# Waits moved, the last two groups' jobs halved, and the end taken tile by tile, in a sparse graph attention layer

## The chip, the cores and the metric

One NeuronCore of a Trainium2 chip runs the whole kernel. The metric is the device time of one execution in microseconds. A step, a job and a group are words of the kernel and are told below.

## The reference

One transformer layer over a graph of 4096 nodes of 256 features, 8 heads of 32, in float32. The adjacency matrix is very sparse, and its first rows are the fullest.

```python
mask = adj.astype(jnp.float32) + jnp.eye(n)
q, k, v = [(h @ W.T + b).reshape(n, 8, 32) for W, b in ((Wq, bq), (Wk, bk), (Wv, bv))]
scores = jnp.einsum('nhd,mhd->hnm', q, k) / sqrt(32)
scores = jnp.where(mask[None] == 0, -1e9, scores)
ctx = jnp.einsum('hnm,mhd->nhd', softmax(scores), v).reshape(n, 256)
h1 = layer_norm(h + ctx @ Wo.T + bo, ln1_g, ln1_b)
ff = relu(h1 @ W1.T + b1) @ W2.T + b2        # 256 -> 1024 -> 256
return layer_norm(h1 + ff, ln2_g, ln2_b)
```

## The kernel before

The kernel writes tables of k, v and q to DRAM, finds each row's few edges in the adjacency matrix, and gathers only the keys and values of these. The 4096 rows are 32 tiles of 128. They are worked in the order ORDER = [5, 6, 4, 3, 2, 7, 1, 0] of groups of four tiles. One pass over one or two tiles is a **step**: steps 0 to 11 take two tiles each, steps 12 to 15 the single tiles 4 to 7, and steps 16 to 18 the tiles 1, 2 and 3, whose rows are fuller. Tile 0 (TILE0), the fullest, has no step of its own: its pieces are set beside steps 2 to 16 (the functions with a 0 in their name). Its weighted sum sum0_pe stands in step 16 (SUM0).

In a step, VectorE (DVE) multiplies gathered keys and queries (edge_scores_dve, own_scores_dve), masks them, normalizes (norm_probs_dve, which signals own_probs), and weights and adds the values (own_sum_dve, edge_weight_dve). In between it prepares later steps: find_dve searches a tile of the adjacency, two steps ahead (FIND_INDEX8, L493), and starts_dve, rt_dve, cols_dve and onehot_dve make the lists of the next step. Small matmuls move data between rows and slots: starts_pe, lists_pe, ell_pe, tr_pe, sum_pe. ACT makes the distances (distance_act) from which rt is made, and the exponentials. POOL issues the gathers (gather_aligned, gather_edges), which are DMAs by index. SP issues plain loads and stores, among them one adjacency tile of 2 MB for each search (load_adj), into two buffers in turn.

The second half of the layer is done in **jobs**, one for each finished group: attn (post_pe_attn: output projection and residual), statistics (post_dve_stats), the rstd on POOL, the norm on ACT (post_act_norm), h1 (transposes), eight blocks f of ff (matmul, then a relu on ACT), out (eight matmuls and a residual for each tile), statistics and norm again, and gain, final (POOL) and the store. A job of four tiles works beside the steps of the next group; step_of_job gives a step's job, its place in the group and the group's number of steps. ff_gap, outs_own and outs_before say which parts of a job's matmuls stand in which of six gaps (dense(0) to dense(5)) of a step. So job 5 is spread over steps 12 to 15 and job 6 over steps 16 to 18. The last group makes two jobs of two tiles, b and c, which are done mostly after step 18. Every engine runs its instructions in the order in which the code lists them; an instruction that waits holds up all behind it on its engine.

The end of every engine's program is general(): it waits for a flag and for all stores, reads the flag, and skips a slow path that handles rows with too many edges.

```python
eng.wait_ge(flag_ready, 1)
eng.wait_ge(main["stored"], GROUPS * 16)
eng.wait_ge(JOBS[GROUPS]["stored"], 16)
raised = eng.value_load(flag[0:1, 0:1], min_val=0, max_val=1)
```

## Time and profile before

| | us |
|---|---|
| median of 3 runs (lowest, highest) | 646.56 (646.11, 647.59) |
| the profiled execution | 645.0 |
| its span, from the first to the last instruction | 643.2 |
| before step 0's first product | 96.2 |
| steps 0 and 1, to the start of step 2 | 47.4 |
| steps 2 to 11 | 272.2 |
| steps 12 to 15 | 87.4 |
| from step 16 to the last matmul | 125.1 |
| after the last matmul | 14.9 |

A step is taken to start with its first VectorE product (L584). PE is TensorE, PEld its weight loads, DVE is VectorE, POOL is GpSimd. A float32 matmul shows as two records, so x8 is four matmuls. An operation's idle time before it is followed by what ended it: the engine, the tile written and the line.

### The profile page before, as it was taken

The numbers are of one execution on the slowest core, as the hardware profiler recorded it, in microseconds if no ns is written. First come the engines' busy times: TensorE is split into PE (matmuls) and PEld (weight loads), VectorE is DVE, ScalarE is ACT, GpSimd is POOL, SyncE is SP. The second block draws the span as 40 slices with busy tenths as digits, with TensorE's granted clock in tenths as the row PEclk, the third lists the DMA queues.
The fourth block names the chain that finished last, engine by engine and source line by source line (L and its number), as shares of the span: only waits on it lengthen the run. The fifth ranks groups of instructions, "written<-read, shape, count | busy, mean of one in ns | idle before, by whom it ended". The sixth has DMA issues, their size and how long they took to land.

```text
span 643.2 us, 7652 instructions
## 1 busy us (share of the span) xinstructions
PE 525.8 (82%) x2434; PEld 414.5 (64%) x2434; DVE 480.3 (75%) x1210; ACT 169.9 (26%) x357; POOL 242.8 (38%) x370
## 2 busy tenths in 40 slices
PE   4999868966799889799989985897688949799790
PEld 3888657855468558757856862685347847478680
DVE  0788968986898989999999878968989791642000
ACT  1111301221323341252242334214211123222510
POOL 5010233552333355456534332432544351322222
PEclk9999877997799989899989988979857968799897
DMA  8999695995986879787796644165275423110010
GB/s 305 416 425 390 218 371 171 363 385 224 322 310 238 312 264 352 255 304 278 255 353 221 246 139 179 32 218 204 88 270 209 143 73 91 49 34 0 2 49 19
DMA packets 39211, 141.08 MB, mean 219 GB/s; under 512 B 4856, under 2 KB 15352, under 8 KB 35072
## 3 DMA queue, kind: packets, MB, share of 16 engines
q1 hardware_dynamic: 24320, 95.16, 39.9%
q0 software_dynamic: 13328, 43.55, 19.8%
q10 hardware_dynamic: 1520, 1.85, 0.8%
q8 instruction: 21, 0.34, 0.2%
q14 instruction: 22, 0.18, 0.1%
HBM read 123.74 MB, written 16.80 MB: 219 GB/s over the span
## 4 chain that ended last, share of the span: by engine, by line
DVE 45%; PE 35%; issue 9%; ACT 4%; DMA 4%; POOL 3%; SPq 0%; POOLq 0%; DVEq 0%; ACTq 0%
DVE found L493 14%; PE ps L1018 8%; PE ps L1569 6%; PE ps L1030 6%; PE ps L999 5%; PE ps L989 3%; DVE stats L1084 3%; DMA work<-q_table,row_of 2%; DVE slots L683 2%; DVE slots L670 2%; DVE slots L692 2%; PE ps L823 2%; ACT early L1074 1%; PE ps L865 1%; DMA xT_all<-in_xT 1%
## 5 line engine op out<-in xcount | busy, mean ns | idle before, releaser
L1018 PE MATMUL ps<-xT_all,w 128*128 128x512 f32 (+1 forms) x288 | 133.2, 610 | 12.3 <-ACT xT_all L1064 9.9
L493 DVE FIND_INDEX8 found<-ones,adj_buf 128x8 uint32<-128x4105 int32 (+5 forms) x40 | 138.7, 3467 | 0.0
L1030 PE MATMUL ps<-w,xT_all 128*128 128x256 f32 x512 | 122.9, 395 | 6.2 <-ACT xT_all L1064 3.2
L1030 PEld LDWEIGHTS ps<-w,xT_all 128*128 128x128 f32 x512 | 98.9, 198 | 21.6 <-ACT xT_all L1064 5.0
L1018 PEld LDWEIGHTS ps<-xT_all,w 128*128 128x128 f32 x288 | 57.6, 212 | 62.5 <-issue 46.1
L949 POOL DMA_INDIRECT slots<-kv_table,col_of x54 | 54.6, 1010 | 67.6 <-DVE col_of L567 56.0
L1084 DVE BATCH_NORM_STATS2 stats<-ps 128x6 f32<-128x256 f32 x64 | 22.9, 419 | 61.1 <-PE ps L989 61.1
L1064 ACT ACTIVATE xT_all<-ps,col_table 128x512 f32<-128x512 f32 (+1 forms) x72 | 45.5, 641 | 82.5 <-PE ps L1018 76.5
L1569 PE MATMUL ps<-early,xT_all 128*128 128x256 f32 x256 | 57.6, 387 | 9.3 <-DMA xT_all<-in_xT 9.3
L1569 PEld LDWEIGHTS ps<-early,xT_all 128*128 128x128 f32 x256 | 49.5, 194 | 16.2 <-issue 9.3
L823 PE MATMUL ps<-work,slots 128*128 128x128 f32 x160 | 33.8, 318 | 27.2 <-DVE slots L692 25.3
L1102 POOL TENSOR_TENSOR rstd<-mv,eps_col 128x4 f32<-128x4 f32 (+1 forms) x18 | 6.0, 331 | 127.2 <-DVE mv L1090 127.2
L941 POOL DMA_INDIRECT slots<-kv_table,found x32 | 34.9, 1089 | 46.5 <-DVE found L493 15.3
L823 PEld LDWEIGHTS ps<-work,slots 128*128 128x128 f32 x160 | 27.4, 226 | 30.7 <-DVE slots L692 28.6
L953 POOL DMA_INDIRECT work<-q_table,row_of x40 | 38.1, 952 | 12.9 <-issue 12.9
L893 ACT ACTIVATE xT_all<-ps,col_table 128x256 f32<-128x256 f32 (+1 forms) x38 | 14.4, 431 | 96.9 <-PE ps L824 95.7
L1111 POOL TENSOR_TENSOR early<-early,row_g 128x1024 f32<-128x1024 f32 (+1 forms) x9 | 21.1, 2339 | 47.9 <-DVE slots L692 32.0
L1587 PE MATMUL ps<-early,xT_all 128*128 128x256 f32 x128 | 36.6, 413 | 0.0
L999 PE MATMUL ps<-wo,xT_all 128*128 128x256 f32 x128 | 35.6, 404 | 1.0 <-issue 1.0
L1587 PEld LDWEIGHTS ps<-early,xT_all 128*128 128x128 f32 x128 | 26.9, 210 | 4.5
L824 PE MATMUL ps<-ident,slots 128*128 128x128 f32 x124 | 27.9, 312 | 0.0
L786 PEld LDWEIGHTS ps<-idx_all,work 128*128 128x128 f32 x80 | 13.0, 229 | 19.8 <-DVE work L548 18.8
(165 smaller groups left out, 872.1 us busy)
## 6 DMA issues: line engine op xcount, KB each, us to landing
adj_buf<-in_adj SPq DMA_DIRECT2D x31, 2048.0 KB
xT_all<-in_xT SPq DMA_DIRECT2D x15, 512.0 KB, 21.8
kv_table<-slots POOLq DMA_DIRECT2D x7, 1024.0 KB, 12.1
slots<-kv_table SPq DMA_DIRECT2D x12, 512.0 KB
q_table<-slots POOLq DMA_DIRECT2D x16, 256.0 KB, 8.8
out_dram<-early SPq DMA_DIRECT2D x7, 512.0 KB
q_own<-q_table SPq DMA_DIRECT2D x12, 256.0 KB
slots<-in_adj SPq DMA_DIRECT2D x1, 2048.0 KB, 24.6
```

The costliest lines, as they stand in the source:

```text
L493: last = nc.vector.max_index(dst, ones8[:], part)
L823: nc.tensor.matmul(to, edge_slots(q)[:, c, feats], onehot[q.par][:, c, :], start=(u == 0), stop=False)
L941: nc.gpsimd.indirect_dma_start(to, None, kv_dram, bass.IndirectOffsetOnAxis(ap=idx, axis=0)).then_inc(got_aligned[q.par], 16)
L949: nc.gpsimd.indirect_dma_start(edge_slots(q)[:, u, :], None, kv_dram, bass.IndirectOffsetOnAxis(ap=col_of[q.par][:, u:u + 1], axis=0)).the ...
L953: nc.gpsimd.indirect_dma_start(q_edge[q.par][:, u, :], None, q_dram[q.no // 2], bass.IndirectOffsetOnAxis(ap=row_of[q.par][:, u:u + 1], ax ...
L999: nc.tensor.matmul(to, q["ctxT"][:, k, j * P:(j + 1) * P], wo[:, k, :], start=(k == 0), stop=False)
L1018: last = nc.tensor.matmul(ps[:, q["bank"] + f % 2, 0:q["g"] * P], w1[:, k, f * P:(f + 1) * P], q["h1T"][:, k, :], start=(k == 0), stop=(k ...
L1030: nc.tensor.matmul(to, q["ffT"][:, f, j * P:(j + 1) * P], w2[:, f, :], start=(f == 0), stop=False)
L1064: nc.scalar.activation(q["ffT"][:, f, :], ps[:, q["bank"] + f % 2, 0:q["g"] * P], ACT.Relu, bias=bias_1[:, f:f + 1]).then_inc(q["ff"], 1)
L1084: last = nc.vector.bn_stats(q["stats"][k][:, j, :], tile_out(q, q["bank"] + 2 * k, j))
L1569: last = nc.tensor.matmul(ps[:, kv_bank(i, part), j * D:(j + 1) * D], xT_all[:, c, k, r * P:(r + 1) * P], wqkv[:, k, (1 + part) * D:(2 + p ...
L1587: last = nc.tensor.matmul(to, xT_all[:, c, k, r * P:(r + 1) * P], wqkv[:, k, 0:D], start=False, stop=(k == KC - 1))
```

## The change

- The last two groups that have jobs beside steps are treated alike: group 6 (tiles 4 to 7) makes two jobs of two tiles, in the two halves of the job buffers, each beside two steps (14 and 15, 16 and 17), and group 7 makes job 8 (b, beside step 18 and after) and the last job (c). MAIN = 9 counts the jobs on the main signals. Job 5 of four tiles is now beside steps 12 and 13.
- TensorE: lists_pe of the next step stands between two halves of attn; in the last two steps tr_pe stands before gap 2; sum0_pe stands before sum_pe; step 18 has no ff.
- VectorE: the first statistics of a job stand behind norm_probs_dve.
- ACT: the second norm of a job stands behind distance_act of the next step.
- POOL: gather_edges stands before the q stores of gap 2. In the steps that are "apart" (11, 13 and 15) gain waits for own_probs of that step and final for own_probs of the next, both before gather_edges.
- SP: two adjacency loads wait for step 0's gathers. Q_BEFORE is 6 instead of 4.
- The end: out of job c signals for each tile, and VectorE does its second norm, gain and final itself (last_dve), with one power on POOL (last_pool). The flag is made before that out, and the wait for the stores stands behind the reading of the flag.

```diff
+JOBS = [job(GROUP, GROUP * ORDER[n], 0, POST, main) for n in range(GROUPS - 2)]
+for g, at in ((GROUPS - 2, 0), (GROUPS - 2, 2), (GROUPS - 1, 0)):
+    JOBS.append(job(2, GROUP * ORDER[g] + at, at, POST, main))
+JOBS.append(job(2, GROUP * ORDER[-1] + 2, 2, 0, post_signals("e_")))
...
     act.wait_ge(acc_ps, q.b + 1)
-    if step_of_job(q)[1] == 0:
-        wait(act, main["attn_ps"], q.group)
+    wait(act, main["attn_ps"], ctx_free(q.b))
...
+    if js[0] == 0:
+        pe.wait_ge(ctx_sem, ctx_value)
+        pe.wait_ge(q["x_biased"], n + 1)
+        wait(pe, q["ff"], n * FC)
+    for j in js:
         to = tile_out(q, q["bank"], j)
         for k in range(KC):
...
             pe.wait_ge(q["ff"], (n + 1) * FC)
...
-        to = tile_out(q, q["bank"] + 2, j)
+        to = ps[:, q["bank"] + 2 + j, 0:D] if each else tile_out(q, q["bank"] + 2, j)
         for f in range(FC):
             nc.tensor.matmul(to, q["ffT"][:, f, j * P:(j + 1) * P], w2[:, f, :], start=(f == 0), stop=False)
         last = add_residual(to, q["h1b"], j)
-        if j == q["g"] - 1:
+        if each or j == q["g"] - 1:
             last.then_inc(q["out_ps"], 1)
...
+def last_dve(dve, q, j):
+    y, o, moments, r = ps[:, q["bank"] + 2 + j, 0:D], q["out"][:, j, :], q["mv"][1][:, j, :], q["rstd"][1][:, j:j + 1]
+    dve.wait_ge(q["out_ps"], j + 1)
+    nc.vector.bn_stats(q["stats"][1][:, j, :], y).then_inc(q["link2"], 1)
+    dve.wait_ge(q["link2"], j + 1)
+    nc.vector.bn_aggr(moments, q["stats"][1][:, j, :]).then_inc(q["mv2"], 1)
+    dve.wait_ge(q["mv2"], j + 1)
+    nc.vector.tensor_scalar(r, moments[:, 1:2], EPS, None, ALU.add).then_inc(q["plink2"], 1)
+    dve.wait_ge(q["rstd2"], j + 1)
+    nc.vector.tensor_scalar(o, y, moments[:, 0:1], r, ALU.subtract, ALU.mult).then_inc(q["norm2"], 1)
+    dve.wait_ge(q["norm2"], j + 1)
+    nc.vector.tensor_tensor(o, o, rows["g2"][:], ALU.mult).then_inc(q["mul2"], 1)
+    dve.wait_ge(q["mul2"], j + 1)
+    nc.vector.tensor_tensor(o, o, rows["be2"][:], ALU.add).then_inc(q["final"], 1)
+def last_pool(pool, q, j):
+    r = q["rstd"][1][:, j:j + 1]
+    pool.wait_ge(q["plink2"], j + 1)
+    nc.gpsimd.tensor_tensor(r, r, neg_half[:, 0:1], ALU.pow).then_inc(q["rstd2"], 1)
 def wide(name, g):
...
     with eng.If(raised > 0):
+        eng.wait_ge(main["stored"], MAIN * 16)
+        eng.wait_ge(JOBS[MAIN]["stored"], 2 * 16)
         path(eng)
     eng.wait_ge(flag_ready, 1)
...
 def step_of_job(q):
-    same = [p for p in STEPS if p.group == q.group]
-    return q.group - 1, q.b - same[0].b, len(same)
+    return q.b // 2 - 1, q.b % 2, 2 if q.b < NB - 1 else 1
...
-def count_of(g):
-    return len([p for p in STEPS if p.group == g])
...
+    return 2 * n + 2 if n < MAIN - 1 else NB - 2
+def ctx_free(i):
+    return {NB - 3: MAIN - 2, NB - 2: MAIN - 1}.get(i, i // 2 if i % 2 == 0 and i <= 2 * GROUPS - 4 else 0)
+def finished(q):
+    return step_of_job(q)[0] - 1
+def apart(q):
+    return step_of_job(q)[1] == 1 and finished(q) >= 0 and q.b + 2 < NB and STEPS[q.b + 2].T == 1
+Q_BEFORE = 6
...
-    return ((11,), (), (12, 13), (14,), (15,), ())[gap] if i == 1 else ()
+        return ((6,), (), (7, 8), (9, 10), (11,), ())[gap]
+    return ((12,), (), (13,), (14,), (15,), ())[gap] if i == 1 else ()
...
-        return (((), (), (), (), (), (0, 1)), ((2, 3), (4,), (5, 6, 7), (), (), ()))[place][gap]
-    if count == 3:
-        return (((), (), (), (), (), (0, 1)), ((2,), (), (3, 4), (5,), (), ()), ((6,), (7,), (), (), (), ()))[place][gap]
-    return (((), (), (), (), (), ()), ((0, 1), (), (2, 3), (4,), (), ()), ((5,), (), (6, 7), (), (), ()), ((),) * 6)[place][gap]
+    if count == 1:
+        return ()
+    return (((), (), (), (), (), (0, 1)), ((2, 3), (4,), (5, 6, 7), (), (), ()))[place][gap]
 def outs_own(place, count, gap):
-    if count == 2:
-        return {(1, 3): (0, 1)}.get((place, gap), ())
...
-def outs_before(place, g, gap):
-    if place or g < 2:
+    return {(1, 3): (0, 1)}.get((place, gap), ())
+def outs_before(place, n, gap):
+    if place or JOBS[n - 1]["g"] < GROUP:
         return ()
-    if count_of(g - 1) < 4:
-        return {2: (2,), 3: (3,)}.get(gap, ())
-    return {2: (3,)}.get(gap, ())
+    return {2: (2,), 3: (3,)}.get(gap, ())
 block = ctx.enter_context(nc.Block())
...
     load_own(sp, STEPS[0])
+    sp.wait_ge(got_edges[STEPS[0].par], 2 * STEPS[0].U * 16)
     load_adj(sp, 4)
     load_adj(sp, 5)
...
         if i + 3 < NB:
             for ti in range(STEPS[i + 3].T):
                 load_adj(sp, STEPS[i + 3].h + ti)
         if i == NB - 2:
-            sp.wait_ge(main["attn_ps"], GROUPS - 1)
-            post_load(sp, JOBS[GROUPS - 1], GROUPS - 1, JOBS[GROUPS - 1]["t"])
-            post_load(sp, JOBS[GROUPS], 0, JOBS[GROUPS]["t"])
-        if place == 1 and n >= 1:
+            sp.wait_ge(main["attn_ps"], MAIN - 1)
+            post_load(sp, JOBS[MAIN - 1], MAIN - 1, JOBS[MAIN - 1]["t"])
+            post_load(sp, JOBS[MAIN], 0, JOBS[MAIN]["t"])
+        if i >= 1 and apart(STEPS[i - 1]):
+            m = finished(STEPS[i - 1])
+            post_store(sp, JOBS[m], m, JOBS[m]["t"])
+        if place == 1 and n >= 1 and not apart(q):
             post_store(sp, JOBS[n - 1], n - 1, JOBS[n - 1]["t"])
-    a, b, c = JOBS[GROUPS - 2], JOBS[GROUPS - 1], JOBS[GROUPS]
-    na, nb, ne = GROUPS - 2, GROUPS - 1, 0
+    a, b, c = JOBS[MAIN - 2], JOBS[MAIN - 1], JOBS[MAIN]
+    na, nb, ne = MAIN - 2, MAIN - 1, 0
     post_store(sp, a, na, a["t"])
     post_store(sp, b, nb, b["t"])
-    post_store(sp, c, ne, c["t"])
+    for j in range(2):
+        sp.wait_ge(c["final"], j + 1)
+        sp.dma_start(out_rows[:, c["t"] + j, :], c["out"][:, j, :]).then_inc(c["stored"], 16)
...
             post_pool_rstd(pool, JOBS[n], n, 0)
+        if i >= 1 and apart(STEPS[i - 1]):
+            pool.wait_ge(own_probs, i + 1)
+            post_pool_final(pool, JOBS[finished(STEPS[i - 1])], finished(STEPS[i - 1]))
+        if apart(q):
+            pool.wait_ge(own_probs, i + 1)
+            pool.wait_ge(s_weights, 16 * WEIGHT_DMAS)
+            post_pool_gain(pool, JOBS[n - 1], n - 1)
+        if soon:
+            gather_edges(pool, soon)
         for p in q_pairs(i, 2):
             store_q(p)
-        if soon:
-            gather_edges(pool, soon)
         if 0 <= i - GATHER0 < PIECES0:
             gather_edges(pool, TILE0, (2 * (i - GATHER0), 2 * (i - GATHER0) + 1))
...
             post_pool_gain(pool, JOBS[n - 1], n - 1)
             post_pool_final(pool, JOBS[n - 1], n - 1)
         if place == 0 and n >= 1:
             post_pool_rstd(pool, JOBS[n - 1], n - 1, 1)
...
-    post_pool_rstd(pool, a, na, 1)
     post_pool_gain(pool, a, na)
     post_pool_final(pool, a, na)
     post_pool_rstd(pool, b, nb, 1)
     post_pool_gain(pool, b, nb)
     post_pool_final(pool, b, nb)
-    post_pool_rstd(pool, c, ne, 1)
-    post_pool_gain(pool, c, ne)
-    post_pool_final(pool, c, ne)
+    for j in range(2):
+        last_pool(pool, c, j)
     general(pool, general_pool)
...
         if i == NB - 1:
-            post_act_x(act, JOBS[GROUPS - 1], GROUPS - 1)
-            post_act_x(act, JOBS[GROUPS], 0)
+            post_act_x(act, JOBS[MAIN - 1], MAIN - 1)
+            post_act_x(act, JOBS[MAIN], 0)
         dense(0)
         if i + 1 < NB:
             distance_act(act, STEPS[i + 1])
+        if place == 1 and n >= 1:
+            post_act_norm(act, JOBS[n - 1], n - 1, 1)
         dense(1)
         probs_act(act, q)
         if i == SOFTMAX0:
             probs0_act(act)
         dense(2)
-        if place == 0 and n >= 0:
+        if place == 0 and n >= 0 and i < NB - 1:
             post_act_norm(act, now, n, 0)
         edge_exp_act(act, q)
+        if i == NB - 1:
+            post_act_norm(act, now, n, 0)
         if i == WEIGHTS0:
             edge_exp0_act(act)
-        if place == 0 and n >= 0:
+        if place == 0 and n >= 0 and i < NB - 1:
             post_act_h1(act, now, n)
         dense(3)
-        if i == NB - 1:
-            post_act_norm(act, JOBS[GROUPS - 1], GROUPS - 1, 0)
+        if i == SUM0:
+            ctx0_act(act)
         ctx_act(act, q)
         dense(4)
-        if i == SUM0:
-            ctx0_act(act)
         dense(5)
+        if i == NB - 1:
+            post_act_h1(act, now, n)
         if place == 0 and n >= 0:
             post_act_h1_bias(act, now, n)
-        if place == count - 1 and q.group < GROUPS - 1:
-            post_act_x(act, JOBS[q.group], q.group)
-        if place == 0 and n >= 1:
-            post_act_norm(act, JOBS[n - 1], n - 1, 1)
-    a, b, c = JOBS[GROUPS - 2], JOBS[GROUPS - 1], JOBS[GROUPS]
-    na, nb, ne = GROUPS - 2, GROUPS - 1, 0
-    post_act_h1(act, b, nb)
-    post_act_ff(act, b, nb, range(0, 2))
+        if place == 1 and i // 2 < MAIN - 1:
+            post_act_x(act, JOBS[i // 2], i // 2)
+    a, b, c = JOBS[MAIN - 2], JOBS[MAIN - 1], JOBS[MAIN]
+    na, nb, ne = MAIN - 2, MAIN - 1, 0
+    post_act_ff(act, b, nb, range(0, 3))
     post_act_norm(act, c, ne, 0)
-    post_act_ff(act, b, nb, range(2, FC))
+    post_act_ff(act, b, nb, range(3, FC))
+    post_act_norm(act, a, na, 1)
     post_act_h1(act, c, ne)
-    post_act_h1_bias(act, b, nb)
-    post_act_ff(act, c, ne, range(0, 4))
-    post_act_norm(act, a, na, 1)
+    post_act_ff(act, c, ne, range(FC))
     post_act_h1_bias(act, c, ne)
-    post_act_ff(act, c, ne, range(4, FC))
     post_act_norm(act, b, nb, 1)
-    post_act_norm(act, c, ne, 1)
     general(act, general_act)
 @block.tensor
...
     starts_pe(pe, TILE0)
-    for i in range(1, Q_BEFORE):
+    for i in range(1, 4):
         project_q(i)
     lists_pe(pe, TILE0)
+    for i in range(4, Q_BEFORE):
+        project_q(i)
     starts_pe(pe, b1_)
...
         ell_pe(pe, q)
+        if n == MAIN - 1:
+            pe.wait_ge(ctx0_ready, 1)
         if place == 0 and n >= 0:
-            post_pe_attn(pe, now, n, ctx_ready, job_ctx_ready(n))
-        dense(1)
+            post_pe_attn(pe, now, n, ctx_ready, job_ctx_ready(n), range(now["g"] // 2))
         if soon:
             lists_pe(pe, soon)
+        if place == 0 and n >= 0:
+            post_pe_attn(pe, now, n, ctx_ready, job_ctx_ready(n), range(now["g"] // 2, now["g"]))
+        dense(1)
         if 0 <= i - SCORE0 < PIECES0:
             ell0_pe(pe, i - SCORE0)
         if i == WEIGHTS0:
             tr0_pe(pe)
-        dense(2)
+        if i + 2 < NB:
+            dense(2)
         tr_pe(pe, q)
-        if place == 0 and n >= 0:
+        if i + 2 >= NB:
+            dense(2)
+        if place == 0 and n >= 0 and i < NB - 1:
             post_pe_h1(pe, now, n)
         dense(3)
-        if i == NB - 1:
-            pe.wait_ge(ctx0_ready, 1)
-            post_pe_attn(pe, JOBS[GROUPS - 1], GROUPS - 1, ctx_ready, NB - 2)
-        sum_pe(pe, q)
-        dense(4)
         if i == SUM0:
             sum0_pe(pe)
+        sum_pe(pe, q)
+        if i == NB - 1:
+            post_pe_h1(pe, now, n)
+        dense(4)
         dense(5)
         if i + 2 < NB:
             starts_pe(pe, STEPS[i + 2])
-    a, b, c = JOBS[GROUPS - 2], JOBS[GROUPS - 1], JOBS[GROUPS]
-    na, nb, ne = GROUPS - 2, GROUPS - 1, 0
+    a, b, c = JOBS[MAIN - 2], JOBS[MAIN - 1], JOBS[MAIN]
+    na, nb, ne = MAIN - 2, MAIN - 1, 0
+    post_pe_ff(pe, b, nb, (0, 1))
     post_pe_attn(pe, c, ne, ctx_ready, NB)
-    post_pe_h1(pe, b, nb)
-    post_pe_ff(pe, b, nb, range(FC))
+    post_pe_ff(pe, b, nb, range(2, FC))
     post_pe_h1(pe, c, ne)
-    post_pe_ff(pe, c, ne, range(0, 4))
-    post_pe_out(pe, b, nb, range(2))
-    post_pe_ff(pe, c, ne, range(4, FC))
-    post_pe_out(pe, c, ne, range(2))
+    post_pe_out(pe, b, nb, (0,))
+    post_pe_ff(pe, c, ne, (0, 1))
+    post_pe_out(pe, b, nb, (1,))
+    post_pe_ff(pe, c, ne, range(2, FC))
     pe.wait_ge(flag_link, 3)
     nc.tensor.matmul(ps[:, POST, 0:2], ones_col[:], flag_f[:, 0:1].to_broadcast([P, 2]), start=True, stop=True).then_inc(flag_ps, 1)
+    for j in range(2):
+        post_pe_out(pe, c, ne, (j,), each=True)
     general(pe, general_pe)
 @block.vector
...
             rt_dve(dve, soon)
-        if place == 0 and n >= 0:
-            post_dve_stats(dve, JOBS[n], n, 0)
         masked_dve(dve, q)
...
         norm_probs_dve(dve, q)
+        if place == 0 and n >= 0:
+            post_dve_stats(dve, JOBS[n], n, 0)
         if later:
...
     nc.vector.tensor_tensor(limit[:], limit[:], start_of[:], ALU.subtract).then_inc(flag_link, 1)
-    post_dve_stats(dve, b, nb, 0)
     post_dve_stats(dve, c, ne, 0)
-    post_dve_stats(dve, a, na, 1)
     dve.wait_ge(flag_link, 1)
     t0, t1 = TILE0.u0, TILE0.u0 + TILE0.U
     nc.vector.tensor_tensor(bad[:, 1, 0:t0], found[:, 0:t0, FOUND - 1], limit[:, 0:t0], ALU.is_le)
...
     dve.wait_ge(flag_link, 2)
     nc.vector.tensor_reduce(flag_f[:], flat(bad[:]), AX_X, ALU.max).then_inc(flag_link, 1)
     post_dve_stats(dve, b, nb, 1)
-    post_dve_stats(dve, c, ne, 1)
     dve.wait_ge(flag_ps, 1)
     nc.vector.tensor_scalar(flag[:], ps[:, POST, 0:1], 0.0, None, ALU.is_gt).then_inc(flag_ready, 1)
+    for j in range(2):
+        last_dve(dve, c, j)
     general(dve, general_dve)
```

## Rows read from the trace of the kernel before

**Rows 1.** The page, busy time and share of the span of engines.

```profile
PE 525.8 (82%) x2434; PEld 414.5 (64%) x2434; DVE 480.3 (75%) x1210; ACT 169.9 (26%) x357; POOL 242.8 (38%) x370
```

**Rows 2.** Busy time by stretch; last PEclk, DMA share, GB/s.

```profile
core 0: us, PE busy (x) PEld busy (x) DVE busy (x) ACT busy (x) POOL busy (x), PEclk, DMA share, GB/s
96.20:143.60 47.40, 38.80 (x189) 33.37 (x187) 40.80 (x88) 11.57 (x25) 22.83 (x26) 0.91 0.83 302
143.60:415.80 272.20, 233.65 (x1076) 175.42 (x1076) 248.23 (x553) 82.53 (x165) 118.84 (x125) 0.92 0.71 253
415.80:503.20 87.40, 70.26 (x297) 52.46 (x298) 74.81 (x214) 20.27 (x47) 37.31 (x37) 0.80 0.58 200
503.20:560.10 56.90, 42.16 (x207) 32.48 (x205) 33.77 (x100) 16.04 (x35) 18.68 (x23) 0.82 0.28 81
560.10:628.30 68.20, 61.88 (x310) 51.91 (x310) 15.80 (x47) 20.21 (x46) 18.25 (x22) 0.97 0.06 20
628.30:643.20 14.90, 0.12 (x2) 0.03 (x1) 1.05 (x5) 1.02 (x2) 3.72 (x6) 0.68 0.06 21
```

**Rows 3.** Waits of VectorE, 90 to 143.65: total us, times, longest.

```profile
DVE work L584 <- DMA work<-q_table,row_of: 8.4, 3, 5.0
```

**Rows 4.** The same view, 143.65 to 415.8.

```profile
DVE stats L1084 <- PE ps L989: 8.4, 4, 4.7
DVE work L548 <- ACT work L875: 4.6, 2, 2.6
```

**Rows 5.** The same view, 415.8 to 503.2.

```profile
DVE stats L1084 <- PE ps L989: 5.2, 1, 5.2
```

**Rows 6.** The same view, 503.2 to 628.4, VectorE, then TensorE.

```profile
DVE bad L540 <- PE ps L779: 12.1, 1, 12.1
DVE p_edge L660 <- PE ps L806: 11.7, 2, 6.9
...
PE ps L823 <- DVE slots L692: 9.2, 2, 7.1
```

**Rows 7.** The timeline, ff (L1018) and out (L1030): start us, us.

```profile
383.89 3.68 PE L1018 MATMUL ps<-xT_all,w 128*128 128x512 f32 x8
...
451.02 6.19 PE L1018 MATMUL ps<-xT_all,w 128*128 128x512 f32 x8
...
600.52 3.72 PE L1018 MATMUL ps<-xT_all,w 128*128 128x256 f32 x16 [1.11 <-ACT xT_all L1047]
...
612.15 3.62 PE L1030 MATMUL ps<-w,xT_all 128*128 128x256 f32 x16
```

**Rows 8.** Groups of TensorE's instructions, 415.8 to 503.2, then 503.2 to 560.1.

```profile
L1030 PE MATMUL ps<-w,xT_all 128*128 128x256 f32 x80 | 22.8, 449 | 0.4 <-ACT xT_all L1064 0.4
L1018 PE MATMUL ps<-xT_all,w 128*128 128x512 f32 x32 | 21.9, 842 | 0.0
...
L865 PE MATMUL ps<-work,slots 128*128 128x128 f32 x56 | 8.6, 326 | 0.8 <-ACT xT_all L893 0.8
```

**Rows 9.** The timeline, POOL's gain beside VectorE in step 11; L512 in step 12.

```profile
410.70 2.34 POOL L1111 TENSOR_TENSOR early<-early,row_g 128x1024 f32<-128x1024 f32 x1 [14.00 <-DVE slots L692]
410.73 2.33 DVE L512 CAST aligned_idx<-idx_all 128x2 uint32<-128x2 f32 x1
...
440.40 0.17 DVE L512 CAST aligned_idx<-idx_all 128x2 uint32<-128x2 f32 x1
```

**Rows 10.** The chain that ended last: gathers of steps 0 and 1.

```profile
83.58 12.58 DMA work<-q_table,row_of
...
116.54 3.48 DMA work<-q_table,row_of
```

**Rows 11.** The timeline, POOL: a gather's issue; the last final.

```profile
495.51 0.94 POOL L949 DMA_INDIRECT slots<-kv_table,col_of  x1 [0.30 <-issue]
...
633.21 1.26 POOL L1115 TENSOR_TENSOR early<-early,row_be 128x512 f32<-128x512 f32 x1
```

**Rows 12.** The page, DMA issues: KB each, median us to landing.

```profile
out_dram<-early SPq DMA_DIRECT2D x2, 256.0 KB, 2.2
```

94 lines of the change are left out of this document (41 added, 53 removed).

## The prediction

> **What bounds the kernel now.** First the page: TensorE is busy 82% and VectorE 75% of the span [rows 1], so neither is a plain bound, and the question is which one is waited for where. So next the busy time by stretch, cut at the starts of steps [rows 2]. Steps 2 to 11 take 272.2 us with VectorE busy 248.2 (91%): VectorE sets the pace, TensorE (233.7, 86%) follows closely. Steps 12 to 15 take 87.4 us with 74.8 and 70.3. From step 16 to the last matmul, 125.1 us, VectorE has 49.6 us of work and TensorE 104.0: there TensorE is the bound, and it idles 21.1 us on top. The last 14.9 us hold almost no TensorE work. Then the waits by stretch [rows 3 to 6]: places where the pace is broken, which the new order can mend. Last, single instructions: what a job costs TensorE [rows 7, 8], what a POOL operation does to VectorE [rows 9], the gathers [rows 10, 11] and the end [rows 11, 12].
>
> **The sum has five parts**, against the profiled execution (645.0 us, span 643.2; the median of the runs, 646.56, is 1.6 higher, and the forecast adds that).
>
> **A. Steps 0 and 1.** SP now waits for step 0's edge gathers before it loads two more adjacency tiles, and POOL issues gather_edges before the q stores of gap 2. VectorE waited 8.4 us in three waits for gathers [rows 3], 5.0 of them in step 0, where the last gather landed 12.6 us after its issue; a later one took 3.5 [rows 10]. The 12.6 is a shared DMA: 4 MB of adjacency were loading. Held back, they start some 9 us later, when the first search that needs them is still 10 us away, and 2 MB at the 302 GB/s of this stretch [rows 2] take 7, so that is hidden, by 3 us only. The other two waits (3.4) go with the earlier issue. Q_BEFORE 4 to 6 moves two q pairs in front of step 0, into TensorE time that waited for VectorE; POOL's stores, and behind them step 1's aligned gather, wait for them, but that gather waited for a q store before too. Bounds 3 and 8.4; I take 7.
>
> **B. Steps 2 to 11.** post_dve_stats(…, 0) moves behind norm_probs, so VectorE no longer stands before attn: 8.4 us in four waits [rows 4]. lists_pe(soon) now stands behind half of attn. A tile of it has four records of the form of out (16 take 3.62 [rows 7]) and a residual of 0.4, so 1.3: the half is done 2.6 us after ell, about when VectorE has made rt. What is late instead is h1 (rstd, norm and h1T follow statistics that start after own_probs), and it lands in time in which TensorE waits for edge_weighted. post_act_norm(…, 1) moves behind distance_act: of the 4.6 us for ACT's distance [rows 4] one norm, some 1.9, can go; ff(2, 3) stay in front. The apart rule moves gain and final of step 11 under the search. Before, they ran beside small VectorE operations: the cast L512 took 2.33 us, until L1111 ended, against 0.17 elsewhere [rows 9]; two such blocks are 4.2 us. What can go: 8.4 + 1.9 + 4.2 = 14.5. TensorE would then be busy 91%, and its own lateness stays; I take 12, bounds 4 and 17.
>
> **C. Steps 12 to 15.** Here the split of the jobs works. Costs at full clock [rows 7]: a tile of out 3.62 and the residual, 3.9; one f of a four-tile ff 3.68 / 2 = 1.84, so 14.7 a job; attn 1.3 a tile; h1 about 1. Before, steps 16 to 18 carry one tile of job 5's out (3.9) and all of the four-tile job 6 (6.3 + 14.7 + 15.6): 40.5. After, they carry one two-tile job (18.5) in its place, so 22.0 us of TensorE work go to steps 12 to 15: 70.3 + 22.0 = 92.3 us for 87.4. But there 32 records of 512 columns took 21.9 us [rows 8], 14.7 at full clock, and 80 of 256 took 22.8, 18.1 at full clock: 11.9 us are half clock (6.19 against 3.68 for the same eight [rows 7]; granted clock 0.80 [rows 2]). Work without gaps keeps it up: 80.4, plus some 5 of waits. VectorE: 74.8 busy, less 4.2 of the lock in step 13, plus 1.0 for one more set of statistics. One new wait: in steps 11, 13 and 15 POOL's gathers queue behind own_probs and the 2.3 us gain, in 12, 14 and 16 behind final. In step 15 six gathers of 0.94 + 0.30 [rows 11] end 9.8 us after own_probs and land some 2.5 later; step 16 begins 9.1 after it. Those 3.2 us are about what the freed wait (5.2 [rows 5]) leaves over. I take 0, bounds -8 and +10.
>
> The matmuls of ff are now 256 wide for two more jobs. The rows price this at nothing: 16 records of 256 take 3.72, 8 of 512 take 3.68 [rows 7]. The Trainium skill speaks against it (TensorE: Matmul & The Clock Gate, Back-to-back issue gap: with weight loads about 81 ns at 128 columns, 131 at 512). A straight line puts 256 at 98, an estimate by which two halves cost half as much again. The measured rows decide, and rival 6 is what is left.
>
> **D. Step 16 to the last matmul, 125.1 us.** TensorE's work was 104.0; 22.0 have left: 82.0. Half clock adds little here (sum0's 56 records 8.6 us [rows 8]) and mostly stays. The idle 21.1 was made by order: sum0 ran after sum(16) and before starts (VectorE stood 12.1 us), and ff and out stood before tr in steps 17 and 18 (11.7) [rows 6]. Now sum0 runs while TensorE waited 7.1 us for edge_weighted [rows 6], tr of steps 17 and 18 goes before gap 2, and step 18 has no dense work. What stays idle: step 18's chain of tr, exp, weights, sum and h1 (6), step 16's norm before h1 (3), the joints of the end (4), where norm of job a still stands before out b. 82 + 13 = 95, so 30 less. Bounds 15 (the moved work, with part of it lost to new gaps) and 38.
>
> **E. After the last matmul, 14.9 us** [rows 2]. Before: 6.1 us from 628.3 to the end of final at 634.47 [rows 11], over two tiles and three engines; then store, landing (2.2 [rows 12]), the flag read and branch, 8.7. After: one tile, mostly on VectorE: bn_stats, half of what two tiles took, 0.4, aggregate 0.1, add 0.1, pow 0.6, three operations of 256 columns at 0.4, gaps: 2.8. So 3.3 less. The wait for stored moves behind the flag read, which hides the landing: 2.2. Together 5.5, bounds 3 and 7.
>
> **Sum:** 7 + 12 + 0 + 30 + 5.5 = 54.5; 645.0 - 54.5 = 590.5, and with the 1.6 of the median 592.
>
> **Rivals.**
> 1. TensorE is the bound as soon as VectorE is freed. For it: 86% busy already in steps 2 to 11, more work than time in 12 to 15. Against: much of that excess is clock. B gives 4, D 18 (C's surplus runs into step 16): 7 + 4 + 0 + 18 + 5.5 = 34.5, so 612. Chance 0.22.
> 2. POOL stands in the way. If gathers behind gain and final take 5 us to land rather than 2.5, four steps are late by 2.5 each: 10 us, 602. Or its operations, released by the same instruction as the search, hold the search up as they held the cast: six times 2.3, 606. The Trainium skill has such a rule (SBUF — State Buffer, Who interferes with whom: the first to issue holds the shared pair for its whole instruction), and the cast agrees with it; whether a search is such an operation neither says. Chance 0.13.
> 3. The clock. The granted clock is 0.80 and 0.82 in the two stretches with gaps and 0.97 where TensorE is dense [rows 2]. If it stays near the latter everywhere, C gives 8 and B 17: 579. Chance 0.13.
> 4. Slower: TensorE at its 1.2 GHz level. 174.3 us of work lie between step 12 and the last matmul, some 158 at full clock. If new gaps keep it at half clock all through, it costs 6.19 / 3.68 of that, 265 us, and with 20 of idle 285 against 212.5 now: 72.5 more, 24.5 of it back from A, B and E, so 695. It decides from about 55% of that work at half clock; now it is some 15%. Chance 0.04.
> 5. The waits move and nothing comes of it: VectorE's work is unchanged, and every removed wait comes back as one for TensorE, also at the end. 645 to 648. The idle beside a named order speaks against it. Chance 0.02.
> 6. Half-wide matmuls cost half as much again: 7.3 us over the ff of both jobs (14.7 / 2), 599. Against: 3.72 and 3.68. Chance 0.02.
>
> The forecast itself has 0.44, with 583 to 601 as its own range. The cases span 579 to 612; with the bounds of C and D the range is 575 to 616, and rivals 4 and 5 and the far ends of 1 and 3 lie outside. A measurement of this kernel can tell some 0.2% (1.3 us) from no change: faster 0.94, same 0.02, slower 0.04.
>
> **What would show it.** A: no wait for gathers in steps 0 and 1. B: no wait of the statistics for attn, no 2.3 us casts; steps 2 to 11 in 260 us. C: steps 12 to 15 in 82 to 95, TensorE over 90% busy, clock above 0.9, 2 to 4 us of wait for a gather at step 16. D: the 12.1 and both tr waits gone, 95 us to the last matmul. E: 9 to 10 us after it. Wrong would be a granted clock still at 0.8, searches stretched by POOL, or VectorE waiting for adjacency loads.

## The result and the profile after

The changed kernel takes 619.32 us (617.81 to 622.48, 4 runs) where the kernel before took 647.08 beside it: ratio 0.957, 95% interval 0.952 to 0.962. That is faster by 27.8 us. The forecast was 592.0, with a range from 575 to 616: the sign was right, the gain was half of the 54.5 us forecast.

The page of the kernel after, busy times and granted clock in 40 slices [rows 1]:

```profile
PE 520.4 (84%) x2466; PEld 419.9 (68%) x2466; DVE 475.0 (77%) x1218; ACT 171.8 (28%) x369; POOL 243.2 (39%) x376
...
PEclk9999898987899979989797989877999897978898
```

Busy time by stretch, cut at the same places as before: the start of steps 0, 2, 12 and 16, the last matmul's end, the end [rows 2]:

```profile
91.20:134.14 42.94, 35.63 (x177) 31.47 (x176) 40.63 (x90) 9.06 (x21) 19.52 (x22) 0.92 1.02 405
134.14:411.11 276.97, 235.28 (x1049) 174.51 (x1048) 244.83 (x554) 83.64 (x166) 120.30 (x126) 0.91 0.70 249
411.11:508.12 97.01, 88.58 (x452) 73.06 (x450) 73.73 (x227) 29.65 (x68) 44.08 (x47) 0.93 0.53 181
508.12:610.80 102.68, 81.58 (x429) 71.76 (x427) 47.89 (x140) 30.59 (x75) 34.81 (x47) 0.90 0.19 59
610.80:618.30 7.50, 0.19 (x2) 0.00 (x0) 2.16 (x6) 0.00 (x0) 0.56 (x1) 0.65 0.12 38
```

Set against the parts of the sum (the last column is e16 below, the fastest complete kernel of this study, in its one profile):

| part | forecast | after | best |
|---|---|---|---|
| A, to the start of step 2 | -7 | -9.5 | -9.3 |
| B, steps 2 to 11 | -12 | **+4.8** | -12.4 |
| C, steps 12 to 15 | 0 | **+9.6** | +6.2 |
| D, step 16 to the last matmul | -30 | -22.4 | -22.5 |
| E, behind it | -5.5 | -7.4 | -7.3 |
| sum | -54.5 | -24.9 | -45.3 |

B alone is 16.8 us off, C 9.6 and D 7.6. A and E gave 4.4 more than forecast.

In B, VectorE's work fell by 3.4 us, but the stretch grew. The waits in it, VectorE's first, then TensorE's and ScalarE's (us in total, times, longest):

```profile
DVE stats L1090 <- PE ps L991: 6.7, 5, 3.2
DVE total_p L645 <- issue: 6.3, 2, 3.3
DVE total_p L645 <- ACT scores L883: 5.6, 2, 3.3
...
PE ps L788 <- DVE work L550: 21.2, 8, 4.6
...
ACT xT_all L1070 <- PE ps L1023: 53.7, 32, 6.6
```

Two of them are new: before, TensorE waited 0.3 us for rt in this stretch, and VectorE did not wait for the exponentials (L645, 11.9 us in both rows; that the first is one too is read from its place). ScalarE's wait for ff was 32.4 us before. VectorE's for attn, which the change was to remove, is 6.7 us where it was 8.4. L788 is lists_pe, L550 is rt on VectorE. TensorE now arrives at the lists eight times before rt is there, 21.2 us in all. The timeline of step 9 (an odd step: no attn, so nothing but ell stands ahead of the lists) shows the rest:

```profile
329.91 0.54 PE L800 MATMUL ps<-work 128*128 128x48 f32 x4
...
334.55 0.47 DVE L550 TENSOR_SCALAR work<-work,half 128x128 f32<-128x128 f32 x2
...
335.08 1.03 PE L788 MATMUL ps<-idx_all,work 128*128 128x9 f32 x4 [4.62 <-DVE work L550]
...
335.95 3.76 PE L1023 MATMUL ps<-xT_all,w 128*128 128x512 f32 x4
...
339.75 0.69 ACT L1070 ACTIVATE xT_all<-ps,col_table 128x512 f32<-128x512 f32 x1 [6.56 <-PE ps L1023]
...
340.34 0.31 ACT L883 ACTIVATE scores<-scores 128x144 f32<-128x144 f32 x1
340.68 0.41 DVE L645 TENSOR_REDUCE total_p<-scores 128x16 f32<-128x144 f32 x1 [3.31 <-ACT scores L883]
```

TensorE stands idle from 330.5 to 335.1, then makes the lists and ff 4. Four records of ff 4 take 3.76 us, half the rate of [rows 7] (eight in 3.68). The granted clock, the third value from the end, says why: 1.00 ahead of the pause, 0.50, the 1.2 GHz level, in the lists and ff 4 behind it.

```profile
320.00:330.40 10.40, 10.33 (x42) 6.33 (x42) 10.16 (x27) 4.41 (x8) 4.51 (x8) 1.00 0.97 352
335.08:339.71 4.63, 4.63 (x9) 2.56 (x10) 2.09 (x11) 0.00 (x0) 1.90 (x2) 0.50 0.53 182
```

ScalarE's program has ff 4's ReLU ahead of the exponentials, so these wait too, and VectorE, which had the scores ready at 336.1, gets them at 340.7.

### The profile page after: what moved, and what is told of

Read it like the earlier page. It is cut to its first block, busy times and chain, and to the rows that moved or that the text cites. A ratio compares the mean times of both kernels' runs of the same rounds, so it can differ in the third digit from the quotient of the medians.

```text
span 618.3 us, 7757 instructions
## 1 busy us (share of the span) xinstructions
PE 520.4 (84%) x2466; PEld 419.9 (68%) x2466; DVE 475.0 (77%) x1218; ACT 171.8 (28%) x369; POOL 243.2 (39%) x376
## 4 chain that ended last, share of the span: by engine, by line
PE 45%; DVE 33%; issue 9%; DMA 4%; POOL 3%; ACT 3%; another core or an unknown queue 1%; POOLq 0%; ACTq 0%; SPq 0%; DVEq 0%
PE ps L1023 11%; PE ps L1036 9%; DVE found L495 8%; PE ps L1606 6%; PE ps L1003 4%; DMA work<-q_table,row_of 3%; PE ps L1624 3%; PE ps L991 3%; DVE stats L1090 2%; DVE slots L602 2%; PE ps L788 2%; PE ps L825 2%; PE ps L1622 2%; DVE slots L672 2%; DVE slots L685 1%
## 5 line engine op out<-in xcount | busy, mean ns | idle before, releaser
L1036 PE MATMUL ps<-w,xT_all 128*128 128x256 f32 x512 | 120.8, 391 | 5.5 <-ACT xT_all L1070 2.1
L1023 PEld LDWEIGHTS ps<-xT_all,w 128*128 128x128 f32 x320 | 65.7, 215 | 51.7 <-issue 39.7
L1070 ACT ACTIVATE xT_all<-ps,col_table 128x512 f32<-128x512 f32 (+1 forms) x80 | 47.9, 601 | 98.5 <-PE ps L1023 93.8
L1606 PEld LDWEIGHTS ps<-early,xT_all 128*128 128x128 f32 x256 | 49.5, 195 | 16.0 <-issue 9.2
L1090 DVE BATCH_NORM_STATS2 stats<-ps 128x6 f32<-128x256 f32 x62 | 22.4, 419 | 34.6 <-PE ps L991 34.6
L894 ACT ACTIVATE xT_all<-ps,col_table 128x256 f32<-128x256 f32 (+1 forms) x38 | 14.4, 430 | 110.5 <-PE ps L826 110.5
L1003 PE MATMUL ps<-wo,xT_all 128*128 128x256 f32 x128 | 39.6, 439 | 5.3 <-issue 3.0
L825 PE MATMUL ps<-work,slots 128*128 128x128 f32 x160 | 31.1, 297 | 12.5 <-DVE slots L694 9.9
L1138 POOL TENSOR_TENSOR early<-early,row_g 128x1024 f32<-128x1024 f32 (+1 forms) x9 | 18.3, 2031 | 58.1 <-DVE slots L694 23.9
L788 PE MATMUL ps<-idx_all,work 128*128 128x9 f32 (+1 forms) x80 | 13.4, 279 | 29.4 <-DVE work L550 29.2
L825 PEld LDWEIGHTS ps<-work,slots 128*128 128x128 f32 x160 | 25.0, 207 | 14.2 <-DVE slots L694 11.7
L788 PEld LDWEIGHTS ps<-idx_all,work 128*128 128x128 f32 x80 | 12.3, 221 | 31.5 <-DVE work L550 31.4
L1003 PEld LDWEIGHTS ps<-wo,xT_all 128*128 128x128 f32 x128 | 25.2, 218 | 8.4 <-issue 4.7
## 6 DMA issues: line engine op xcount, KB each, us to landing
xT_all<-in_xT SPq DMA_DIRECT2D x14, 512.0 KB, 22.5
kv_table<-slots POOLq DMA_DIRECT2D x7, 1024.0 KB, 12.1
```

The costliest lines, as they stand in the source:

```text
L788: last = nc.tensor.matmul(lists_out(q)[:, u, :], rt[q.par][:, u, :], lists(q)[:, u, q.A:q.room + 2], start=True, stop=True)
L825: nc.tensor.matmul(to, edge_slots(q)[:, c, feats], onehot[q.par][:, c, :], start=(u == 0), stop=False)
L1003: nc.tensor.matmul(to, q["ctxT"][:, k, j * P:(j + 1) * P], wo[:, k, :], start=(k == 0), stop=False)
L1023: last = nc.tensor.matmul(ps[:, q["bank"] + f % 2, 0:q["g"] * P], w1[:, k, f * P:(f + 1) * P], q["h1T"][:, k, :], start=(k == 0), stop=(k ...
L1036: nc.tensor.matmul(to, q["ffT"][:, f, j * P:(j + 1) * P], w2[:, f, :], start=(f == 0), stop=False)
L1070: nc.scalar.activation(q["ffT"][:, f, :], ps[:, q["bank"] + f % 2, 0:q["g"] * P], ACT.Relu, bias=bias_1[:, f:f + 1]).then_inc(q["ff"], 1)
```

## The experiments

Every ratio is to the kernel before, run beside it on the same chip. B, C, D are the stretches above, from one profiled execution of each kernel. The same kernel gave 0.926 on one chip and 0.931 on another (e10 and e16), so a difference of 3 us between two experiments says little.

### The lists back, the norm back, and single parts

e1_lists_back:

```diff
-if place == 0 and n >= 0: post_pe_attn(..., range(now["g"] // 2))
-if soon: lists_pe(pe, soon)
-if place == 0 and n >= 0: post_pe_attn(..., range(now["g"] // 2, now["g"]))
+if place == 0 and n >= 0: post_pe_attn(pe, now, n, ctx_ready, job_ctx_ready(n))
 dense(1)
+if soon: lists_pe(pe, soon)
```

> The changed kernel with one part undone: attn whole, then gap 1, then lists_pe of the next step, as before. Theory 1 (lists_pe in front of half of attn and of ff 4 makes TensorE wait for rt, 21.2 us in steps 2 to 11, drops its clock, and so holds ff 4's relu, which stands before the exponentials on ACT, and the second half of attn): VectorE's waits for the exponentials (11.9 us) and the statistics (6.7 us) in steps 2 to 11 shrink to below 4 us together, TensorE's wait for rt to below 5, and the kernel takes 600 to 608 us against 619. Theory 2 (the norm that now stands before the exponentials on ACT holds them): the waits for the exponentials stay, 615 to 620.

Measured: 602.36 us, ratio 0.933 (0.926 to 0.941): 17 us less than the changed kernel. B takes 263.9, TensorE waits 3.1 us for rt in it, and VectorE's wait for the exponentials is gone. Step 9 in its timeline:

```profile
320.41 0.54 PE L800 MATMUL ps<-work 128*128 128x48 f32 x4
...
320.79 1.95 PE L1023 MATMUL ps<-xT_all,w 128*128 128x512 f32 x4
...
324.29 0.61 PE L788 MATMUL ps<-idx_all,work 128*128 128x9 f32 x4 [1.55 <-DVE work L550]
...
325.33 0.32 ACT L883 ACTIVATE scores<-scores 128x144 f32<-128x144 f32 x1 [1.04 <-DVE scores L638]
```

The same ff 4 fills the gap, takes 1.95 us, and the exponentials wait for nothing but VectorE.

e2_norm_back puts ScalarE's second norm back to the end of the even step (`post_act_norm(act, JOBS[n - 1], n - 1, 1)` behind `post_act_x` at place 0).

> The changed kernel with another part undone: the second norm of a job stands at the end of the first step of a pair on ACT, not behind distance_act of the second. Theory 1: the exponentials are held by ff 4's relu and not by the norm, so the waits for them stay near 12 us, VectorE waits for distance_act again by some 2 us a time, and the time is 619 to 626 us. Theory 2: the waits for the exponentials go, 608 to 613.

Measured: 618.98 us, 0.954 (0.950 to 0.960), no change from 619.3, and VectorE's wait for the exponentials stays:

```profile
DVE total_p L645 <- ACT scores L883: 11.8, 4, 3.3
```

The norm on ScalarE is not what holds them.

e3_lists_alone: the kernel before with the same order of attn, lists and gap 1 and nothing else.

> The kernel before with one part of the change alone: lists_pe of the next step between two halves of attn and before gap 1. Theory 1: TensorE waits for rt in the second step of each pair (4 to 5 us, then ff 4 at half clock) and VectorE for what follows: slower than before by 5 to 15 us, 652 to 662. Theory 2: nothing of note, 643 to 649.

Measured: 671.50 us, 1.038 (1.031 to 1.045), slower than before, and by more than expected, 24 us. Its waits in B:

```profile
DVE stats L1087 <- PE ps L989: 21.6, 5, 6.5
DVE total_p L643 <- ACT scores L881: 10.0, 4, 3.3
...
PE ps L786 <- DVE work L548: 17.5, 8, 4.6
```

With the statistics still ahead of the masking, VectorE also waits for the second half of attn, 4.3 us a group. The order is worst there. That the changed kernel's late statistics hide part of it is the likely reading; the changed kernel has other parts too.

e4_stats_alone: the kernel before with `post_dve_stats(dve, JOBS[n], n, 0)` behind `norm_probs_dve`.

> The kernel before with another part alone: the first statistics of a job behind norm_probs_dve. The forecast's step B: VectorE's waits for attn (8.4 us in steps 2 to 11, 5.2 in step 12, 3.0 in step 16) nearly vanish, and since TensorE idles 13 us before sum_pe in steps 2 to 11 most of it is gained: 632 to 638. Rival (TensorE is the bound as soon as VectorE is freed): the waits come back at starts_pe and tr_pe, 643 to 647.

Measured: 643.07 us, 0.994 (0.991 to 0.997): 4.1 us, less than half of what was expected, and what the rival said. Waits in B, TensorE's and VectorE's:

```profile
PE ps L1008 <- ACT xT_all L1074: 16.5, 5, 5.0
DVE slot_of L556 <- PE ps L786: 6.8, 3, 5.3
```

The 8.4 us of [rows 4] went to the next thing that attn makes late, the lists behind it, and to h1, which waits for a norm whose statistics start later.

### GpSimd's order

e5_gather_first is e1 with gather_edges ahead of gain and final in the apart steps:

```diff
+if soon: gather_edges(pool, soon)
 if i >= 1 and apart(STEPS[i - 1]): ... post_pool_final(...)
 if apart(q): ... post_pool_gain(...)
-if soon: gather_edges(pool, soon)
```

> The first experiment's order (lists behind attn and the first gap), and GpSimd issues the gathers of the step after next ahead of the pending gain and final of a group, in place of behind them. Theory G (the gathers of the last steps are late because they stand behind these two and behind their waits): the 8.0 us that VectorE waited for gathers at the starts of three of the steps 14 to 17 go to under 3, and the time from 602.4 to 595 to 599. Rival (TensorE is the bound there, VectorE's wait is only where its slack shows): the waits for gathers go, waits for TensorE take their place, 601 to 604.

Measured: 606.41 us, 0.936 (0.932 to 0.941), against e1's 0.933. The wait for gathers from step 12 on fell from 8.0 to 2.4 us and nothing came of it. TensorE's waits, e1's row and then this kernel's:

```profile
PE ps L825 <- DVE slots L694: 4.5, 2, 3.5
```

```profile
PE ps L825 <- DVE slots L694: 9.6, 4, 3.5
```

TensorE's wait for VectorE's weighted values (L825 is sum_pe) grew by 5.1 us in its place. The late gathers cost nothing that can be measured here.

e6_apart_off is e1 with `apart()` always False.

> The first experiment's order, and GpSimd makes gain and final of every group at the old place, so that none is held for the next step's softmax to end. If that placing is worth what the prediction gave it (three norms of about 4.2 us of VectorE's wait for GpSimd saved each), the gathers come in time (8.0 us back) but 12.6 come in waits of VectorE beside GpSimd's work: 605 to 608. Rival (the placing costs as much as it saves, since it is what holds the gathers): 601 to 604 or less.

Measured: 612.23 us, 0.944 (0.940 to 0.949): 9.9 us slower than e1 by the medians, 7 by the ratios, and above the range expected. The gathers come in time, as in e5, where that won nothing. Step 11 alone takes 34.8 us, in e1 30.7. The cast of [rows 9] is back, twice, 2.34 and 2.33 us long (min, median, max in ns):

```profile
L514 DVE CAST aligned_idx<-idx_all x7: 169/169/2336, 366.3 to 520.8; 128x2 uint32<-128x2 f32 x5, 128x3 uint32<-128x3 f32 x2
```

In the kernel after, gain and final run beside searches, and the searches are not held: final beside one of step 14 for 1.2 us, gain beside one of step 15 for nearly all of it, and in step 12 a search that began while final was running. The forms of these searches took 2560 and 1227 ns on average before.

```profile
429.06 2.35 POOL L1142 TENSOR_TENSOR early<-early,row_be 128x1024 f32<-128x1024 f32 x1
...
430.98 1.23 DVE L495 FIND_INDEX8 found<-ones,adj_buf 128x8 uint32<-128x1032 int32 x1
...
474.16 2.56 DVE L495 FIND_INDEX8 found<-ones,adj_buf 128x8 uint32<-128x2312 int32 x1
475.54 2.35 POOL L1142 TENSOR_TENSOR early<-early,row_be 128x1024 f32<-128x1024 f32 x1
...
495.88 2.56 DVE L495 FIND_INDEX8 found<-ones,adj_buf 128x8 uint32<-128x2312 int32 x1
...
495.98 2.35 POOL L1138 TENSOR_TENSOR early<-early,row_g 128x1024 f32<-128x1024 f32 x1 [4.70 <-DVE scores L657]
```

### Start, end, and all but the split

e7_start_alone: the kernel before with part A (`sp.wait_ge(got_edges[...], ...)` ahead of the adjacency loads, gather_edges ahead of store_q, `Q_BEFORE = 6`).

> The kernel before with the change's start alone: the load queue waits for step 0's gathers before adjacency, gathers ahead of the q stores, six q pairs before the start with two of them behind the lists. In the changed kernel steps 0 and 1 were over 9.4 us sooner; if that comes from this part alone and is kept to the end, 636 to 640. Rival (what the start wins, steps 2 to 15 give back, as their waits are for TensorE): 643 to 646.

Measured: 635.61 us, 0.981 (0.976 to 0.985), 11.6 us. Nothing is given back later: B takes 271.1 and C 87.5 us, as before.

e8_end_alone: the kernel before with part E (last_dve, last_pool, a store for each tile, the flag read ahead of the wait for stores).

> The kernel before with the change's end alone: the last group's out, statistics, norm and store tile by tile, and the flag read ahead of the wait for the stores. From the last matmul to the end of the span 14.9 us before and 7.6 in the changed kernel; if it is this part, 639 to 641 and 7 to 8.5 us behind the last matmul. Rival (the shorter tail came from the smaller jobs and their own buffers): 644 to 646.

Measured: 640.58 us, 0.989 (0.984 to 0.994), 6.6 us; 7.3 us are left behind the last matmul.

e12_all_but_split: both and e4 together, four-tile jobs to the end, lists at the old place.

> The kernel before with the change's start, statistics and end together, groups of four tiles up to the end and the lists at the old place. If the three add (11.6, 4.1 and 6.6 us measured alone): 623 to 627, and what the first experiment has beyond it, 21 to 25 us, is the split of the last groups with the order of the last steps. Rival (the parts win the same waits): 629 to 633.

Measured: 623.00 us, 0.964 (0.960 to 0.967). The three add up: 22.3 us alone, 23.5 together (the kernel before took 646.5 beside it). So e1's remaining 20.6 us are the split of the jobs with the order of the last steps, ScalarE's norm (nothing by e2) and GpSimd's order, which e6 puts at 7 to 10.

### Where the lists cost

By the starts of steps, after against e1: the even steps 2 to 10 differ by 1.4 us in sum, the odd ones 3 to 11 by 11.7. Two kernels take the places apart:

```diff
 # e9_whole_attn            # e10_gap_back
 post_pe_attn (whole)       post_pe_attn (half 1)
 lists_pe                   lists_pe        if attn here
                            post_pe_attn (half 2)
 dense(1)                   dense(1)
                            lists_pe        if no attn here
```

> The changed kernel with attn whole in front of the lists, the lists still in front of the first gap's ff. Changed kernel against the first experiment by step starts: the even steps 2 to 10 differ by 1.4 us in sum, the odd steps 3 to 11 (no attn there, ff 4 in the gap) by 11.7. Theory P (the price is the lists ahead of the gap's ff 4 in the odd steps, which goes half clock and holds ReLU and exponentials): little won here, 614 to 618. Rival (the halves of attn, as the prediction placed the risk, start the delay that the odd steps only show): 603 to 607. Both in part: 608 to 613.

> The changed kernel with the lists between the halves of attn kept in the even steps, and behind the first gap's ff in the odd steps. Theory P (see the run before): nearly all of the first experiment's 17 us, 603 to 606. Rival (the halves of attn): 614 to 618.

Measured: e9 620.12 us, 0.953 (0.948 to 0.959); e10 600.64 us, 0.926 (0.923 to 0.930). Each lies just outside the range of theory P, on the side away from the rival: the halves of attn cost nothing that can be measured, and the loss comes from the odd steps, where the lists went ahead of ff 4.

e11_stats_first is e1 with the first statistics ahead of masked_dve, as before.

> The first experiment with VectorE's first statistics ahead of the masking, as in the kernel before. Its TensorE waits 16.6 us in five of the steps 2 to 11 for ScalarE's norm, which waits for these statistics; before, VectorE waited 3.6 to 4.7 us a group for attn there. Theory S (the move is worth its 4.1 us alone, no more once the rest is changed): 604 to 608. Rival (without the late lists TensorE is ahead, the statistics find attn done, and the norm comes sooner): 598 to 601.

Measured: 611.02 us, 0.945 (0.942 to 0.949): 8.7 us slower than e1. The move of the statistics, worth 4.1 alone, is worth about twice that with the rest, and neither number expected came out.

e13_ff4_later is the changed kernel with ff 4 in gap 2: `((2, 3), (), (4, 5, 6, 7), (), (), ())`.

> The changed kernel as it is, lists between the halves of attn and ahead of the first gap in both kinds of step, but ff 4 of the odd steps stands in the next gap (behind the exponentials on ScalarE, ahead of the transposes of the probabilities on TensorE), in place of the first. Theory R (the price is ff 4's ReLU, which ScalarE runs ahead of the exponentials and which waits for TensorE, which waits for VectorE): nearly all won, 600 to 606. Rival T (TensorE's wait for rt and its slower clock are the price): 613 to 619.

Measured: 616.47 us, 0.951 (0.946 to 0.955), 3 to 4 us less than the changed kernel. The exponentials come in time now. In its step 9, and among its waits of VectorE in B:

```profile
332.16 1.03 PE L788 MATMUL ps<-idx_all,work 128*128 128x9 f32 x4 [4.63 <-DVE work L550]
...
333.19 0.32 ACT L883 ACTIVATE scores<-scores 128x144 f32<-128x144 f32 x1 [2.91 <-DVE scores L638]
...
334.03 8.21 PE L1023 MATMUL ps<-xT_all,w 128*128 128x512 f32 x16
```

```profile
DVE p_edge L662 <- PE ps L808: 10.8, 4, 3.6
```

What had been a wait for exponentials is one for tr (L808), which now stands behind four blocks of ff. So ScalarE's order is at most a small part of the price: TensorE stands idle with ff 4 ready, has it still to do afterwards, and whichever consumer comes next is late by it.

The idle time by itself is not the price either. In B TensorE waits 15.1 us for rt in e14 below, which has e10's order, and 3.1 in e1, and B is 263.5 and 263.9 us. There the wait stands behind ff 4, not ahead of it.

### Steps 12 to 15 and the last steps

Each of the four runs here starts from e10. e16_same_again is e10 unchanged, run beside e17.

> The last kernel but two (lists behind the gap in the odd steps, 600.6 us) with half of group 5's ff left out: of the two parts of the sum over the model's width only the first is computed for this group, in steps 12 and 13, about 7.2 us of TensorE at full clock. Theory C (TensorE bounds steps 12 to 15, as its 86.7 busy us of 93.9 say): steps 12 to 15 take 87 to 90 us, the time 594 to 597. Rival (VectorE's chain bounds them): under 2 us, 599 to 601.

> The kernel of 600.6 us with the out of the first job of two tiles taken from step 17 (ahead of its weights' sum) to step 18 behind its scores and attn. In step 18 VectorE waited 5.0 us for TensorE's scores behind this out, and TensorE later 3.5 us for the last weights. Theory D (that wait is at the head of the end's chain): TensorE's 3.5 us and part of the others go, 594 to 598. Rival (TensorE's 50 busy us in the last 60 set the end, the waits come elsewhere): 599 to 602.

> The kernel of 600.6 us once more, unchanged, as the measure for the run beside it: 598 to 603.

> The kernel of 600.6 us with half of the ff of group 5 and of the first two jobs of two tiles left out (one of the two parts of the sum over the model's width is not computed for them), 7.2 + 3.6 + 3.6 us of TensorE at full clock in steps 12 to 17. Theory C (TensorE bounds these steps): 8 to 13 us less than the run beside it, steps 12 to 15 at 84 to 88 us. Rival (VectorE's chain or the gathers bound them, TensorE's busy time only filled what was free): 0 to 4 us less. Between them if both stand close to each other: 5 to 7 less.

The edits, e14 with group 5 alone in place of the three, and e15:

```diff
-for k in range(KC):
+kc = 1 if any(q is JOBS[m] and n == m for m in (5, 6, 7)) else KC   # e17
+for k in range(kc):
...
+if n != MAIN - 2: post_pe_out(pe, now, n, outs_own(place, count, gap))          # e15
+if n == MAIN - 1: return {1: (0, 1)}.get(gap, ())          # in outs_before
```

Measured: e14 600.18 us, 0.926 (0.922 to 0.930), not the 594 to 597 of theory C: steps 12 to 15 take 89.1 us, inside its 87 to 90, but the time is that of e10 (0.926) and 3 us under that of e16 (0.931), both on other chips. e16 601.75 us, 0.931 (0.928 to 0.934). e17 596.22 us, 0.921 (0.918 to 0.924), 5.5 less than e16, steps 12 to 15 in 88.2. So 14.4 us less of TensorE's work are worth 5.5: TensorE and VectorE stand close together there, the third case that was expected. e15 604.81 us, 0.931 (0.926 to 0.936), no gain: VectorE's wait of 5.0 us for the scores of step 18 is gone from its trace, but one of 7.1 for tr (1.3 in e16) has come, so it does not show what the wait alone was worth.

e16's stretches 2 to 11, 12 to 15, 16 to the last matmul:

```profile
134.39:394.22 259.83, 223.86 (x1046) 166.16 (x1046) 244.06 (x555) 83.49 (x166) 120.57 (x126) 0.95 0.74 266
394.22:487.78 93.56, 87.86 (x455) 72.32 (x453) 73.49 (x226) 29.58 (x68) 43.68 (x47) 0.95 0.54 187
487.78:590.40 102.62, 81.62 (x428) 71.68 (x427) 47.79 (x140) 30.64 (x75) 35.20 (x47) 0.90 0.19 59
```

This kernel (e10 and e16), 600.6 and 601.8 us in two sets of runs, beats both: 45 us under the kernel before and 18 under the changed one.

## Why the prediction was wrong

**A held, by 2.5 us more.** No wait for gathers is left in steps 0 and 1, and e7 shows it kept to the end.

**B is the step that failed.** The prediction looked at attn alone: "the half is done 2.6 us after ell, about when VectorE has made rt", and went on to h1. Where there is attn that cost nothing (e10), though rt is later than it says: e16's TensorE waits for it there too, up to 2.5 us. But the same line moves the lists ahead of the gap's ff in the odd steps, where nothing stands between ell and the lists, and this was put at nothing. The trace of before had the price: in steps 3, 5, 7, 9 and 11 rt was ready 1.4, 3.7, 1.7, 3.2 and 2.0 us after ell, and ff 4 stood in that time. Its step 9:

```profile
334.64 0.54 PE L798 MATMUL ps<-work 128*128 128x48 f32 x4
336.11 1.98 PE L1018 MATMUL ps<-xT_all,w 128*128 128x512 f32 x4 [0.92 <-ACT xT_all L1064]
337.87 0.48 DVE L548 TENSOR_SCALAR work<-work,half 128x128 f32<-128x128 f32 x2
```

After, the five steps wait 1.5, 3.5, 4.6, 4.6 and 1.5 us with ff 4 undone, and half the rate comes on top. Against the seven profiles of kernels with the lists behind ff 4 (e1, e5, e10, e14 to e17) TensorE's busy time in B is 7 to 11 us more for the same work, and B 13 to 17 us longer. e9 and e10 show the place, e13 that most of it isn't ScalarE's order. With the lists back B is 259.8 (e16) to 263.9 us; 260 was forecast. The single terms were less right than their sum: the late statistics, put at 8.4, gave 4.1 alone and 8.7 with the rest (e4, e11), GpSimd's placing, put at 4.2 a group, gave 7 to 10 for three groups (e6), and ScalarE's norm, put at 1.9, nothing that can be measured (e2).

**C: the mechanism was right, its size was off.** TensorE is over 90% busy at a clock of 0.93, as forecast, but with 88.6 us, not 80.4. The term that is short is the moved work. In the kernel after, step 12 begins with work of step 11 on TensorE. The timeline of TensorE, and VectorE's first wait, its step 12 having begun at 411.11:

```profile
409.89 3.62 PE L1036 MATMUL ps<-w,xT_all 128*128 128x256 f32 x16
413.35 0.61 PE L991 MATMUL ps<-ident,early 128*128 128x128 f32 x4
413.79 0.39 PE L825 MATMUL ps<-work,slots 128*128 128x128 f32 x2
...
415.36 0.39 PE L826 MATMUL ps<-ident,slots 128*128 128x128 f32 x2
...
415.90 0.16 DVE L542 SCALAR_TENSOR_TENSOR bad<-spill,ps 128x2 f32<-128x2 f32 x1 [3.07 <-PE ps L781]
```

Before, that sum was done at 415.2 and VectorE began step 12 at 415.8. Now it is done at 415.7, VectorE is 4.6 us into step 12, and waits 3.1 us for it. VectorE's lead at the border is a debt of TensorE, and it falls due where TensorE has no room. By forms, C holds 140 records of out where the forecast's eight tiles have 128 (some 2.7 us), and 12 and 11 more records of the two sums than before (4.1 us): of the 8.2 us too little in the prediction these explain 6.8. Half clock that stayed is in it as well: the ff of 256 columns took 9.9 us, 7.4 at the rate of [rows 7]. e17 shows that TensorE's work from step 12 to 17 sets the time in part: 5.5 us of the 14.4 taken out. Where the rest of C's excess comes from isn't settled.

**D: the work was right, the idle time was not.** TensorE's busy time was forecast as 82.0 and is 81.6. The idle time was forecast to fall from 21.1 to 13 and is 21.1 again: the two waits of [rows 6] went (12.1 to 1.2 us, 11.7 to 1.3), and TensorE waits 2.2 to 3.5 us each for what sum, h1, tr and ell of steps 16 to 18 need. The removed waits were VectorE's, and were counted as TensorE's gain. So the 22.4 us of D are the 22.5 us of work that left it, as far as these rows go. Which wait sets the end isn't settled; e15 tried one, and moved it.

**E held, with 7.4 for 5.5**, alone 6.6 (e8).

**The rivals.** Rival 1 (TensorE the bound) gave 612, the nearest of the cases to 619, but not by its own sum: in C and D it is true in part, its 4 us for B had the wrong sign. Rival 2 is half refuted: late gathers there were, of 3.1 and 3.5 us at steps 16 and 17, but free (e5); searches aren't held by GpSimd, 2.56 us with gain beside them. The Trainium skill's rule (SBUF — State Buffer, Who interferes with whom) is narrower than the prediction had it: it names VectorE's two-port modes, with casts among the operations that can enter them, and instructions with two SBUF inputs. The casts agree with it (2.33 us beside GpSimd, 0.17 alone), and it does not name the search. Rival 3: the best kernel has a granted clock of 0.95 in B and C, near its 0.97, but 0.90 in D, and C still takes 6.2 us more than before. Rivals 4 and 5 did not come as stated, with a clock of 0.93 and 0.90 from step 12 on and 27.8 us won; but what each describes, half clock behind new gaps and waits that move to TensorE, is what took B's gain. Rival 6 is refuted by a row of the kernel after, where 24 records of 256 columns take 5.34 us, 3.56 for 16:

```profile
596.16 5.34 PE L1023 MATMUL ps<-xT_all,w 128*128 128x256 f32 x24
```

The range left out what happened, since B's lower bound was a gain of 4: no case had the change itself as the cause of new waits in steps 2 to 11. e3 shows how far it could have gone, 24 us slower. That the total came within 3.3 us of the range owes something to A and E, which gave 4.4 us more than forecast.

## What to carry to other kernels

When a helper moves in a loop with two kinds of turns, cost the move in each kind: what stood between the producer and the helper, and is it still there? Put a wait behind work that is ready, even where its result is wanted early; on an engine with little room the time lost ahead of that work comes back at the next consumer, with a slower clock on top. And where a faster engine leaves one behind that is as busy, count at each border what the second still owes.

## What had not been expected of the hardware

- Short pauses of a TensorE that is otherwise full were followed by its 1.2 GHz level. In the kernel after it waited eight times for rt in steps 2 to 11, and behind seven of these waits the granted clock was between 0.50 and 0.69 over the 3 to 4 us that follow the lists; the shortest of the seven were 1.49 us (steps 3 and 11). Behind that of 1.25 us (step 6) it stayed at 1.00. The fall doesn't come at the same place: behind the 4.63 us of step 7 the lists' four records still took 0.61 us and only ff 4 the half rate (3.66 us), while behind 2.69 us (step 8) the lists took 1.02 already. What decides this wasn't sorted out.
- GpSimd's 2.35 us operation holds VectorE's small cast (2.34 us in place of 0.17) but not FIND_INDEX8, neither where the search came first (2.56 us, 2560 ns on average before) nor where GpSimd did (1.23 us, 1227 ns before). GpSimd's own operation took 2.35 us beside the searches too.
